# Four PSUM banks for relation products, a transferred constant key row and two scrap tiles for row maxima, in a four-layer graph network

## What is computed

```python
# layer 0: weighted neighbour sums of x @ W0
x = layernorm(x + segment_sum((x @ W0)[src_of_edge] * edge_weight) + b0)
# layer 1: twice, with relations r = 0, 1 (the type of an edge)
w = einsum('rb,bio->rio', att, basis)              # 30 bases mixed to 2 weights
gate_r = sigmoid(x @ gate_w[r])
msg_r = (gate_r * x)[col] @ w[r]                   # chosen by edge type
h = relu(segment_sum(msg) + x @ root + bias)       # and again with the second set
# layer 2: degree-normalised sums of x @ W2.T + b2, with a loop at each node
# layer 3: attention over the edges, 8 heads of 64
logits = q[rows] . k[cols] / 8 + att_bias
p = exp(logits - segment_max(logits)[rows])
y = segment_sum(p / denom[rows] * v[cols]);  out = y @ Wo + bo
```

## Time and profile before

| | |
|---|---|
| runs, us | 1229.38, 1230.10, 1231.61 (median 1230.1) |
| profiled execution, us | 1231.27 |
| its span, first to last instruction, us | 1229.5 |
| mean granted TensorE clock | 0.986 of 2.4 GHz |
| instructions | 21718 |
| TensorE, VectorE, ScalarE, GpSimd busy, us | 1167.1, 846.4, 439.7, 365.1 |

### The profile page before, as it was taken

The page is one execution under the profiler, slowest core; times in us unless marked ns, Lnnn a source line. Parts: engine busy times, 40 slices in busy tenths (PEclk is TensorE's granted clock), DMA queues, the critical chain, the costliest instruction groups (busy, mean ns, idle before and its releaser), DMA issues.

```text
span 1229.5 us, 21718 instructions
## 1 busy us (share of the span) xinstructions
PE 1167.1 (95%) x8137; PEld 545.5 (44%) x8138; DVE 846.4 (69%) x1332; ACT 439.7 (36%) x590; POOL 365.1 (30%) x340
## 2 busy tenths in 40 slices
PE   6989999899999989999999999999999899999997
PEld 2334444233444443364445454454333465555553
DVE  7577777344342755652478874657999799899897
ACT  1456666222232212212301003135552355445354
POOL 3034441000350224335555655554557100000000
PEclk9999999999999989999999999999999799999999
DMA  9669995987887988661122212113223566565652
GB/s 312 237 200 324 326 335 149 358 349 260 321 293 273 326 312 309 200 206 3 19 35 36 48 6 70 2 2 45 34 35 58 185 232 228 200 221 197 203 186 111
DMA packets 67490, 222.74 MB, mean 181 GB/s; under 512 B 33200, under 2 KB 38064, under 8 KB 50140
## 3 DMA queue, kind: packets, MB, share of 16 engines
q1 hardware_dynamic: 34846, 156.38, 36.0%
q0 software_dynamic: 28208, 53.10, 18.0%
q10 hardware_dynamic: 4350, 12.07, 2.8%
HBM read 199.90 MB, written 59.92 MB: 211 GB/s over the span
## 4 chain that ended last, share of the span: by engine, by line
PE 46%; DVE 11%; issue 7%; DMA 2%; ACT 2%; ACTq 0%; DVEq 0%
PE PS L1885 13%; PE PS L1837 6%; PE PS L1950 5%; PE PS L2168 4%; PE PS L2155 4%; DVE R L1202 4%; DVE R L1239 4%; PE PS L2037 2%; PE PS L1692 2%; DMA w_d<-R 2%; PE PS L2214 2%; PE PS L1934 2%; PE PS L1921 1%; PE PS L2185 1%; PE PS L1802 1%
## 5 line engine op out<-in xcount | busy, mean ns | idle before, releaser
L833 POOL DMA_INDIRECT bias_d<-R x160 | 267.7, 1673 | 317.7 <-DMA bias_d<-R 224.3
L1885 PE MATMUL PS<-R 128*128 128x512 f16 x900 | 205.8, 381 | 0.0
L799 POOL DMA_DIRECT2D bias_d<-bias_d x159 | 82.6, 526 | 267.5 <-PE PS L1885 123.8
L1648 ACT ACTIVATE R<-PS 128x1024 f32<-128x1024 f32 (+1 forms) x100 | 106.2, 1087 | 110.3 <-PE PS L2155 80.2
L1837 PE MATMUL PS<-W,XX 128*128 128x512 f16 x600 | 134.4, 382 | 5.4 <-DVE R L1031 4.6
L1885 PEld LDWEIGHTS PS<-R 128*128 128x128 f16 x900 | 84.2, 98 | 118.8 <-issue 27.4
L1762 PE MATMUL PS<-R,XX 125*128 125x512 f16 (+2 forms) x612 | 123.1, 343 | 5.5 <-DVE R L947 4.4
L1202 DVE CUSTOM_DVE_ANT_0 R<-PS,R 128x1250 f16<-128x1250 f32 x80 | 116.8, 1460 | 5.5 <-PE PS L2091 2.9
L947 DVE TENSOR_SCALAR R<-W 125x1250 f16<-125x1250 f16 x160 | 89.6, 604 | 37.8 <-PE PS L1762 35.4
L2168 PE MATMUL PS<-R 128*32 128x256 f32 (+1 forms) x1600 | 102.2, 390 | 5.1 <-DVE R L1239 5.1
L2155 PE MATMUL PS<-R 128*128 128x256 f16 (+3 forms) x800 | 100.8, 277 | 6.1 <-DMA R<-R 2.8
(11 more groups left out here) (234 smaller groups left out, 1475.7 us busy)
## 6 DMA issues: line engine op xcount, KB each, us to landing
bias_d<-bias_d POOLq DMA_DIRECT2D x159, 320.0 KB, 5.5
R<-in_basis_s SPq DMA_DIRECT2D x32, 1024.0 KB, 7.6
W<-in_basis_s SPq DMA_DIRECT2D x28, 1024.0 KB, 6.3
W<-bias_d SPq DMA_DIRECT2D x27, 1024.0 KB, 4.9
XX<-bias_d SPq DMA_DIRECT2D x13, 1024.0 KB, 4.9
R<-key_d SPq DMA_DIRECT2D x20, 500.0 KB
R<-R SPq DMA_DIRECT2D x120, 80.0 KB, 4.9
W<-bias_d SPq DMA_DIRECT2D x7, 904.0 KB, 4.6
```

What stands on the lines that cost most here:

```text
L833: pool.indirect_dma_start(bias_d, bass.IndirectOffsetOnAxis(ap=idx[:, c:c + 1], axis=0), attr[:, c, :], None, bounds_check=DUMP + GC * P - ...
L1648: S.activation(ER[n % 4][:, :, 0:w, :].rearrange("p g r u -> p g u r"), PS[:, 2 * (n % 2):2 * (n % 2) + 2, :].rearrange("p a (e r) -> p a ...
L1885: ins = T.matmul(mm_out(SUM_BANK(s, i), D), lhs, rhs, start=n == 0, stop=n == len(terms) - 1)
```

## The change

1. Products of stages 1 and 2 use four banks, 0, 1, 6 and 7 by turns; products 2 and 3 of stage 1 use 4 and 5. A product waits for z_low of the product four before, in stage 3 still two before. New waits on TensorE: xt_made for all tiles ahead of product 6 of stage 1, h_made for all chunks ahead of product 2 of stage 2, and the last two low parts ahead of roots(2) and roots(3).
2. The transpose and the broadcast of the attribute maximum go to unused columns of bank 3. The wait for bdiff_made moves from ahead of roots(0) to the first gates of the second pass, which write bank 3.
3. The constant key row is filled by a transfer on SP, from 128 partitions of 80 numbers that GpSimd sets early. SP issues it ahead of heads_copied(0), after a wait for loops_out. GpSimd's late memset and its wait go.
4. Row maxima write to two scrap tiles by turns; VectorE's wait for its own instruction goes, and it waits for the maximum two before. max_kept gets a wait for all maxima that it reads.

The words "sums of equal edges stay in their plain form" in its description name no edit: nothing of matched or summed is touched.

```diff
+        def ZBANK(s, k, r):
+            m = k * ZRELS[s] + r
+            if s == 3:
+                return m % 2
+            return 2 + m if s == 1 and m in (2, 3) else (0, 1, 6, 7)[m % 4]
...
+            sp.wait_ge(scale_row_made, 1)
+            sp.wait_ge(loops_out, NT)
+            sp.dma_start(KH[DK:DK + 1, :, :].rearrange("u h (k n) -> u (h k) n", n=HEADS * NN // P),
+                         scale_row).then_inc(kone_made, 16)
             for o_ in range(FT):
                 heads_copied(o_)
...
+            pool.memset(scale_row, MSCALE).then_inc(scale_row_made, 1)
 
             pool.wait_ge(zero_out, 16 * ZF)
             for b in range(BATCHES):
-                if b == BATCHES - 1:
-                    pool.wait_ge(loops_out, NT)
-                    pool.memset(KH[DK:DK + 1, :, :], MSCALE).then_inc(kone_made, 1)
...
-                    V.scalar_tensor_tensor(Z[:, r, 1, k, :], mm_out(zi % 2, D), scale, Z[:, r, 0, k, :], ALU.mult,
+                    V.scalar_tensor_tensor(Z[:, r, 1, k, :], mm_out(ZBANK(s, k, r), D), scale, Z[:, r, 0, k, :], ALU.mult,
...
                 dve.wait_ge(s_done, idx + 1)
+                if idx >= 2:
+                    dve.wait_ge(s_used, idx - 1)
                 b0 = 3 * (idx % 2)
-                V.tensor_tensor_reduce(out=junk[:, 0:NODES],
+                V.tensor_tensor_reduce(out=(junk, junk2)[idx % 2][:, 0:NODES],
...
-                dve.wait_ge(s_used, idx + 1)
 
             def max_kept(q):
+                dve.wait_ge(s_used, 4 * NT * (q + 1))
...
                 if i == 0 and layer:
                     pe.wait_ge(gate_made, 2)
+                    pe.wait_ge(bdiff_made, 1)
...
-                    if zi >= 2:
-                        pe.wait_ge(zl_made, zi - 1)
+                    held = 2 if s == 3 else 4
+                    if s == 3 or zi - Z0[s] >= held:
+                        pe.wait_ge(zl_made, zi - held + 1)
+                    if (s, k, r) == (1, 3, 0):
+                        pe.wait_ge(xt_made, NT)
+                    if (s, k, r) == (2, 1, 0):
+                        pe.wait_ge(h_made, CHUNKS)
...
-                    T.transpose(mm_out(7, EC, HEADS), bmax[0:EC, :], ident[0:EC, 0:EC]).then_inc(bmt_done, 1)
+                    T.transpose(PS[0:HEADS, 3, P:P + EC], bmax[0:EC, :], ident[0:EC, 0:EC]).then_inc(bmt_done, 1)
...
                 if p_:
                     pe.wait_ge(h_made, c - FT + 1)
+                elif f >= 2:
+                    pe.wait_ge(zl_made, Z0[1] + RELS * NT - FT + f + 1)
...
             pe.wait_ge(w16_made, 1)
-            pe.wait_ge(bdiff_made, 1)
...
-            pe.wait_ge(kone_made, 1)
+            pe.wait_ge(kone_made, 16)
```

More of the change, by code:

```diff
@@ L293, in gnn_resnorm @@
         o1 += NT
+        junk2 = r1f[:, o1:o1 + NN // 2].bitcast(F16)
+        assert o1 + NN // 2 <= half
         rden = r1f[:, o1:o1 + QUADS * RB].rearrange("p (q r) -> p q r", q=QUADS)
@@ L299, in gnn_resnorm @@
         negative = r2[0:DK, o2 + NN // 2 + P:o2 + NN // 2 + P + DK // 2].bitcast(F16)
+        scale_row = r2[:, o2 + NN // 2 + P + DK // 2:o2 + NN // 2 + P + DK // 2 + HEADS * NN // P // 2].bitcast(F16)
+        assert o2 + NN // 2 + P + DK // 2 + HEADS * NN // P // 2 <= KEPT
         yT = XX[:, NT * D:NT * D + FT * RB].rearrange("p (f n) -> p f n", f=FT)
@@ L434, in gnn_resnorm @@
         kone_made = sem("kone_made")
+        scale_row_made = sem("scale_row_made")
         wo_in = sem("wo_in")
@@ L1070, in _ @@
                     dve.wait_ge(bmt_done, 1)
-                    step(V.tensor_reduce(bmax1[0:HEADS, :], mm_out(7, EC, HEADS), AX.X, ALU.max))
+                    step(V.tensor_reduce(bmax1[0:HEADS, :], PS[0:HEADS, 3, P:P + EC], AX.X, ALU.max))
                     V.tensor_scalar(diag8[0:HEADS, :], ident[0:HEADS, 0:HEADS], bmax1[0:HEADS, :], None,
@@ L1076, in _ @@
                     V.tensor_tensor(attr[0:EC, :, :], attr[0:EC, :, :],
-                                    PS[0:EC, 6, 0:HEADS].rearrange("p (u h) -> p u h", u=1).broadcast_to(
+                                    PS[0:EC, 3, DK:DK + HEADS].rearrange("p (u h) -> p u h", u=1).broadcast_to(
                                         [EC, CH, HEADS]), ALU.subtract).then_inc(bdiff_made, 1)
@@ L1482, in z_high @@
                     scale = dis[:, k:k + 1] if s == 3 else gate[:, k, r:r + 1]
-                    S.activation(Z[:, r, 0, k, :], mm_out(zi % 2, D), ACT.Copy, scale=scale).then_inc(zh_made, 1)
+                    S.activation(Z[:, r, 0, k, :], mm_out(ZBANK(s, k, r), D), ACT.Copy, scale=scale).then_inc(zh_made, 1)
             for i in range(NT):
@@ L1836, in z_tile @@
                     for n, (lhs, rhs) in enumerate(terms):
-                        ins = T.matmul(mm_out(zi % 2, D), lhs, rhs, start=n == 0, stop=n == len(terms) - 1)
+                        ins = T.matmul(mm_out(ZBANK(s, k, r), D), lhs, rhs, start=n == 0, stop=n == len(terms) - 1)
                     ins.then_inc(zz_done, 1)
@@ L1907, in _ @@
                     pe.wait_ge(bmax_made, 1)
-                    T.transpose(mm_out(7, EC, HEADS), bmax[0:EC, :], ident[0:EC, 0:EC]).then_inc(bmt_done, 1)
+                    T.transpose(PS[0:HEADS, 3, P:P + EC], bmax[0:EC, :], ident[0:EC, 0:EC]).then_inc(bmt_done, 1)
                 if k == 8:
                     pe.wait_ge(bdiag_made, 1)
-                    T.matmul(mm_out(6, HEADS, EC), ones[0:HEADS, 0:EC], diag8[0:HEADS, :], start=True,
+                    T.matmul(PS[0:EC, 3, DK:DK + HEADS], ones[0:HEADS, 0:EC], diag8[0:HEADS, :], start=True,
                              stop=True).then_inc(bmb_done, 1)
```

## The result

| | before | changed | changed, again on another chip |
|---|---|---|---|
| runs beside each other, median us | 1230.86 | 1216.68 | 1218.9 (before there 1229.74) |
| lowest to highest, us | 1229.38 to 1237.08 | 1215.64 to 1221.24 | 1215.21 to 1223.8 |
| ratio, 95% interval | | 0.9882 (0.984 to 0.9925) | 0.9918 (0.9887 to 0.9948) |
| profiled execution, span, us | 1231.27, 1229.5 | 1215.64, 1213.7 | 1215.21, 1213.3 |

What follows compares the result with a forecast made beforehand. TensorE, busy 95% of 1229.5 us, was taken as the bound up to the maxima; 2.3 + 3.05 + 1.9 + 2.35 + 2.0 + 1.0 = 12.6 us off the median 1230.1 gave 1217.5 us, 8-in-10 range 1213 to 1223.5.

Steps and rivals of the forecast that it cites:

- Layer 1: Relation products and first roots: four banks gain 2.3 us, the moved bdiff_made wait 3.05, the clock 1.9; together 7.25.
- Does it arrive: Mix stage: the whole 7.25 us of layer 1 passes through, since mixes and their DMA demand move with the first sums.
- rival (a): Mix stage: DMA throughput takes back part of layer 1, 7.25 us becomes 2.3, time 1222.5 us; chance 0.12.
- Layer 2: Layer-2 products: four banks hide TensorE's idle 1.87 and 0.48 us, gain 2.35 us.
- Row maxima: VectorE's 80 maxima without the self-wait: period 1.47 us, 0.035 less each, 2.8 us in all, taken as 2.0.
- The bound of 4.4: Row maxima: upper bound of the gain, 1.09 us of TensorE idle time in each of four stretches, then TensorE bounds.
- Rival (b): Row maxima don't shorten, as the pipeline admits nothing sooner or TensorE is the bound: 1219.5 us; chance 0.05.
- Hand-over: Start of the last stage: bias loads lead the last maxima by 5.6 us instead of 3.5, gain 1.0 us.
- The key row: GpSimd's scatter queue: without the 8.62 us memset the last batch is issued some 6.4 us earlier; the transfer costs 0.
- (c): Hand-over: scatters end last, moving by 6.4 us alone if zero fills held the first one; 1220.2 us, chance 0.03.
- (d): Scatters beside the maxima: VectorE without a break shuts GpSimd out, 2.8 us per pair, 1269 us; chance 0.04.

Runs made afterwards that it cites:

- before_four_banks: Kernel before with only the four banks, the moved transposes and the moved bdiff_made wait: 1221.8 us, ratio 0.9933.
- changed_bdiff: Changed kernel with the wait for bdiff_made ahead of roots(0) again: 1222.58 us, ratio 0.9942.
- changed_two_banks: Changed kernel with relation products on two banks again, moved transposes and moved wait kept: 1222.75 us, ratio 0.9944.
- changed_selfwait: Changed kernel with one scrap tile and VectorE's wait for its own end behind each row maximum again: 1219.77 us, ratio 0.9907.
- before_scrap: Kernel before with two scrap tiles and no VectorE self-wait, two banks kept, small transposes moved: ratio 1.0015.
- light_fewer: changed_fewer with only the first of three value product terms behind the maxima (low parts of tiles 1 to 9 left out): 1217.51 us, ratio 0.9903.
- changed_memset: Changed kernel with the constant key row set by GpSimd's late memset again: 1220.15 us, ratio 0.9914.
- changed_again: Changed kernel once more, no edit, on another chip: 1218.9 us, ratio 0.9918 against the kernel before.
- changed_fewer: Changed kernel without the last 8 of the 160 scatters: 1216.69 us, ratio 0.9905.
- before_key_row: Kernel before with the constant key row by transfer, two banks kept, small transposes moved: ratio 0.9991.
- mrow_act: Changed kernel with the last row of maxima issued on ScalarE's queue, not by SP behind two bias loads: 1220.75 us, ratio 0.9923.

## Why the prediction came out right, step by step

**Layer 1: right in mechanism and size.** 7.31 us of 7.25, and 49.76 us for that stretch in before_four_banks too. changed_bdiff gives back 4.9 (forecast 3.05 + 1.9), changed_two_banks 2.4 (forecast 2.3). Two small misses cancel: the roots took 7.96 us and not the 7.7 of the working, so the clock was worth 1.7 and not 1.9; and each stop costs some 0.15 us more than its idle row (2.41 us for 2.25, 4.89 for 3.05 + 1.68, 2.65 for 2.35). The first scatter came at 400.98; from the forecast's 403 differ the 2.5 us of the untouched first stretch.

**Does it arrive: yes.** The mix stage keeps its length, 154.51 us against 154.85. It is also the place where executions part: over all kernels here it lasts from 150.1 to 155.7 us whatever the edit, so this pair alone would not refute rival (a), which needs 5 us. All profiles together do: the nine with the whole gain of layer 1 have 153.9 us there on average, the three without it 153.2; and before_four_banks takes 8.7 us less, with an interval of 5.5 to 10.9, where (a) leaves 4.6.

**Layer 2: under-sized.** 2.65 us where the clock had held in before, 4.3 where it had not; forecast 2.35, the idle time alone, without the 0.15 us at each of two stops. The sum counted the clock behind the first gap and not behind this one, since the earlier trace rows show 5.34 us behind it.

**Row maxima: mechanism right, size off.** The forecast took a period of 1.47 and dropped a quarter of the rows: 2.0 us. VectorE's own period is 1.39, 0.11 us less and not 0.035, since the next maximum starts with the accumulator read and not 0.08 us after it. That would be 79 x 0.11 = 8.7 us; 2.6 come through. In the last 19 rows TensorE is the bound: three rows with their products take 4.48 us (932.10 to 936.58 in the chain), 1.49 each. Ahead of them the rest goes where a row waits for its scores, though TensorE has some idle time there too (busy 9.3 to 9.5 us of 10 in many stretches): ahead of the scores behind two of the 1.88 us steps it had itself stood 0.52 us for a ScalarE copy (L1603). The bound of 4.4 from TensorE's idle time held. Rival (b), nothing at all, is refuted by changed_selfwait and before_scrap.

**Hand-over: the step that failed.** Forecast was a lead of 5.6 us for the bias loads and a gain of 1.0. The list of SP's queue left out a wait: ahead of the loads SP waits for v_made, the last value copy. In before this ended at 960.65, 1.1 us ahead of the loads that the earlier trace rows show, so the scatters stood alone in sight. Now the last scatter is issued 16.4 us earlier and the copy ends only 14.5 earlier, at 946.16, and the loads follow it at 946.18. The lead is 3.74 us, and the gain 0.2.

This wait is only a part of what the lead fell short by, 1.9 us. The scatters alone, with the 3.07 us from last issue to loads that before shows, would have let the loads go at 945.4, so the copy costs 0.7. The other 1.1 come from the other terms: without the first stretch the maxima were turned 12.9 us earlier and not 11.6, the last scatter came 13.9 earlier and not 13.65. The 1.0 us for a lead of 5.6 was itself too small, a middle between two bounds: light_fewer, with a lead of 5.20, has its row landed in 2.27 us, 1.8 less than before. The over-sized 1.0 and the under-sized maxima nearly cancel, so that the sum is right to a microsecond is in part luck; it is better than its parts.

The lead and the landing belong together. Over all profiles with two loads ahead; the last column is the time from the first maximum to the next scores:

| kernel | lead of the loads | landing of the row | sum | to next scores |
|---|---|---|---|---|
| changed_bdiff | 0.95 | 6.91 | 7.9 | 126.21 |
| changed_memset | 2.17 | 5.48 | 7.7 | 124.80 |
| before_scrap | 2.21 | 5.44 | 7.7 | 124.74 |
| changed_again | 3.41 | 4.36 | 7.8 | 123.57 |
| before | 3.50 | 4.06 | 7.6 | 125.95 |
| changed | 3.74 | 3.88 | 7.6 | 123.18 |
| changed_two_banks | 3.75 | 3.89 | 7.6 | 123.20 |
| changed_fewer | 3.75 | 3.94 | 7.7 | 123.25 |
| before_four_banks | 4.52 | 2.92 | 7.4 | 124.71 |
| changed_selfwait | 4.62 | 2.84 | 7.5 | 124.73 |
| before_key_row | 4.63 | 2.88 | 7.5 | 124.77 |
| light_fewer | 5.20 | 2.27 | 7.5 | 121.92 |

The row lands 7.4 to 7.9 us after the loads were issued, for leads from 0.95 to 5.20 us: in this range whoever holds the loads back (scatters, or the value copies) sets the next scores as much as the maxima do.

**The key row: right in size at its place, little at the end.** 6.6 us on GpSimd; at the next scores 1.2 us alone and 1.1 to 1.6 us with the other parts, by the profiles. In before_four_banks, which has the memset, the scatters happened to be quick and it cost nothing (lead 4.52 us). Its transfer delays nothing: the stretch up to the first maximum is 236.04 us against 236.05.

**Rivals (c) and (d).** (c) happens in some executions, though not by its condition: the first scatter moved with the rest, it is the time of the 160 scatters that varies. Its price of 2.7 us fits changed_bdiff (3.0); in mrow_act the stretch from the first maximum to the end is 7.3 to 7.6 us longer than in the changed kernel's two profiles. (d) is refuted: before and after, half of the 17 spacings of pairs beside the maxima are 5.7 us or less. GpSimd's timeline beside the maxima shows pairs 5.6 us apart with the idle time of the earlier trace rows:

```profile
835.08 1.55 POOL L847 DMA_INDIRECT bias_d<-R  x1 [2.22 <-DMA bias_d<-R]
...
840.71 1.55 POOL L847 DMA_INDIRECT bias_d<-R  x1 [2.23 <-DMA bias_d<-R]
```

**Left open.** Why the clock fell behind a 1.8 us gap in two of four profiles and behind a 2.26 us gap in one of four, and why the mix stage and the scatters vary by some 5 and 14 us from one execution to the next. Of the two comparisons' 14.2 and 10.8 us no run tells which is nearer; the stages give 13.3. No variant beat the changed kernel with all of its work in it.

## What to carry to other kernels

Where two or three chains end within a few microseconds, an edit of one gives back less than it saves at its place: the memset's 6.6 us and the 2.6 us of the maxima became, in single profiles, 1.2 us each at the next scores. A gain of that size doesn't show in the medians of ten runs that spread over 8 us; look for it in the stretch from one fixed point to the next, in several profiles. Before you move what is last, write down every wait ahead of each queued transfer, the met ones too, since the next to last takes over; and when an edit closes a TensorE gap or lightens TensorE, price the granted clock with it.

## What was not expected of the hardware

- A VectorE maximum that writes an accumulator lets the next one start in the same moment as the accumulator read: 1.39 us start to start for instructions of 1.46 us, with no wait between them; 1.50 with one.
- After 3.05 us of idle time the clock fell in all four profiles that have this gap, and 48 matmuls of 384 columns took 9.57 to 9.64 us instead of 7.96. After 1.8 us it fell in two of four (24 matmuls took 7.03 us, else 5.34), after 2.26 us in one of four (48 took 12.21 us, else 10.52). In light_fewer, with TensorE 3.08 to 4.42 us busy in five, it went down to 0.65.
- A transfer of 10 KB lets its successor start 2.3 us after issue when nothing is ahead, and lands 7.4 to 7.9 us after the issue of two 1 MB loads when they are (12 profiles); issued by a second queue behind three loads it took 6.39 us (one profile).
